# A routed expert network: six of eight token tiles moved before the loop starts, running sums by scan, and the later set-up in another order

## The reference, cut to what matters

```python
gates = softmax(xt @ gate_w); top_v, top_i = top_k(gates, 2)      # 8 experts, 2 per token
top_v = top_v / sum(top_v)
h = gelu(einsum('nd,edf->enf', xt, fc_w), approximate=False)      # first block: 128 -> 512 -> 128
eo = einsum('enf,efd->end', h, proj_w)
out = sum(take(eo, top_i) * top_v)
...
gu = einsum('bsd,edh->ebsh', x, w_gate_up); g, u = split(gu, 2)   # fourth block: 128 -> 2 x 512 -> 128
expert_out = einsum('ebsf,efd->ebsd', silu(g) * u, w_down)
return einsum('bse,ebsd->bsd', gate_probs, expert_out)
```

## Time and profile before

| what | value |
|---|---|
| median of three runs | 620.51 us |
| profiled execution, its own time | 617.3 us |
| its span in the profile | 615.6 us |
| PE busy | 537.0 us (87%) |
| DVE busy | 410.1 us (67%) |
| POOL busy | 272.4 us (44%) |
| ACT busy | 239.9 us (39%) |
| mean granted TensorE clock | 0.926 of full |

### The profile page before, as it was taken

How to read it: one execution, slowest core, us unless ns; L and a number is a source line. 1 busy time by engine, 2 the same in 40 slices (tenths; PEclk the granted TensorE clock), 3 DMA queues, 4 the chain that set the end, 5 groups by cost and what they waited for, 6 DMA issues and landing times.

```text
span 615.6 us, 12275 instructions
## 1 busy us (share of the span) xinstructions
PE 537.0 (87%) x3780; PEld 456.0 (74%) x3781; DVE 410.1 (67%) x1482; ACT 239.9 (39%) x551; POOL 272.4 (44%) x505
## 2 busy tenths in 40 slices
PE   4999866998899899999999798989974399999992
PEld 2678553987896599898977675757763199999992
DVE  8878846322357885456689869888887556555573
ACT  3455233543454434444423233455531043334330
POOL 4464373888758108900000010546436368774332
PEclk9999657999997899999989989999995599999996
DMA  9998011322253100000000720004001112221233
GB/s 304 380 311 266 10 52 37 84 73 69 70 163 107 58 1 1 2 1 1 1 1 2 219 56 2 0 2 138 1 2 39 48 50 71 60 61 52 77 109 120
DMA packets 48153, 47.66 MB, mean 77 GB/s; under 512 B 6470, under 2 KB 37603, under 8 KB 47942
## 3 DMA queue, kind: packets, MB, share of 16 engines
q1 hardware_dynamic: 43558, 37.68, 20.5%
q0 software_dynamic: 4544, 9.38, 4.5%
HBM read 27.53 MB, written 19.51 MB: 76 GB/s over the span
## 4 chain that ended last, share of the span: by engine, by line
PE 73%; DVE 20%; issue 4%; ACT 1%; DMA 1%; another core or an unknown queue 1%; DVEq 0%; POOLq 0%; POOL 0%; SPq 0%; ACTq 0%
PE bank L2391 17%; PE bank L2402 10%; PE bank L1987 8%; PE bank L2183 4%; PE bank L2228 4%; PE bank L2267 4%; PE bank L2256 2%; PE bank L1976 2%; PE bank L1977 2%; PE bank L1978 2%; PE bank L1868 2%; PE bank L2325 1%; PE bank L2379 1%; PE bank L2218 1%; DVE stats L1095 1%
## 5 line engine op out<-in xcount | busy, mean ns | idle before, releaser
L2391 PE MATMUL bank<-xT,wcur 128*128 128x128 f32 x936 | 118.6, 277 | 6.6 <-ACT xT L880 3.6
L2391 PEld LDWEIGHTS bank<-xT,wcur 128*128 128x128 f32 x936 | 110.6, 192 | 10.0 <-issue 5.5
L627 POOL TENSOR_SCALAR var_eps<-mv 128x4 f32<-128x4 f32 (+2 forms) x12 | 2.8, 236 | 183.3 <-DVEq L1813 95.8
L684 POOL DMA_INDIRECT yt<-Y,dest_i x62 | 61.3, 989 | 50.7 <-ACT Y L896 32.0
L668 POOL DMA_INDIRECT xw<-XW,slot_i x64 | 63.3, 989 | 43.3 <-ACT xT L880 10.9
L1445 DVE COPY wcur<-WA 128x512 f32 x78 | 36.3, 466 | 50.3 <-PE bank L2391 26.4
L964 ACT ACTIVATE hT<-bank,b_cols 128x512 f32<-128x512 f32 x64 | 44.0, 688 | 63.1 <-PE bank L1978 62.5
L1987 PE MATMUL bank<-WC,hT 128*128 128x128 f32 x512 | 64.1, 280 | 0.0
L1987 PEld LDWEIGHTS bank<-WC,hT 128*128 128x128 f32 x512 | 61.7, 195 | 1.4
L1583 DVE SCALAR_TENSOR_TENSOR X<-bank,G,X 128x128 f32<-128x128 f32 x128 | 36.0, 343 | 32.7 <-PE bank L1987 27.4
L1460 DVE TENSOR_TENSOR hT<-gb,bank 128x512 f32<-128x512 f32 x39 | 26.8, 688 | 41.7 <-ACT gb L885 39.5
(11 more groups left out here) (406 smaller groups left out, 1182.6 us busy)
## 6 DMA issues: line engine op xcount, KB each, us to landing
xw<-pad_rows SPq DMA_DIRECT2D x34, 260.0 KB, 4.4
xrow<-xw SPq DMA_DIRECT2D x78, 65.0 KB
WA<-in_fc_dram SPq DMA_DIRECT2D x16, 256.0 KB, 4.7
YT<-yt SPq DMA_DIRECT2D x16, 256.0 KB, 3.6
WA<-in_pj_dram SPq DMA_DIRECT2D x8, 256.0 KB, 5.2
WB<-in_fc_dram SPq DMA_DIRECT2D x8, 256.0 KB, 4.9
WB<-in_pj_dram SPq DMA_DIRECT2D x8, 256.0 KB, 6.3
X<-in_x_dram SPq DMA_DIRECT2D x2, 512.0 KB, 4.4
```

The source lines that it names most:

```text
L684: pool.indirect_dma_start(out=yt_dram, out_offset=bass.IndirectOffsetOnAxis(ap=dest_i[:, t:t + 1], axis=0), in_=y_slot(layer, t), in_offse ...
L2391: ins = pe.matmul(dst, wcur[:, s4, at:at + P], xT[s4 % 2][:, :], start=True, stop=True)
```

## The change

It does five things.

1. The moves of group 0 are counted by two semaphores: the first six token tiles (SOON, both choices, 12 moves) and the last two (4 moves). The order of the moves is tile by tile with both choices. The loop's table gets a sixth kind, tiles that are filled by these six token tiles, and SP loads the first five loop tiles (SOON_ONLY is 5) after 12 moves instead of 16. The table has 48 segments.
2. Running sums are made by one `tensor_tensor_scan` in place of the doubling steps: in `choices` over 64 bf16 numbers in place of L1312 to L1315, in `table` over 48 f32 numbers in place of the copy, the six steps and a subtraction. The scan runs on over the experts, so PE takes off what came before with two more matmuls (`minus_bf`) in each `ranks`. The copy of the logits (L1305) goes: DVE reads them from PSUM.
3. `table_out` stands before the last reduction of `places`, not behind the `routed` cast.
4. The later set-up in layer 0 stands otherwise: on PE the bias row before `ranks(0)`, half of the values behind it, two of the four score matrices ahead of `ranks(1)`, the other two and the keys behind the table; ACT's 16 key copies come before the first group's exponents; DVE fetches the first four weights ahead of the masks of the values, and splits the bias row after the loop's counts.
5. PE no longer waits for `most_moved`; it warms with 0 matmuls in layer 0 (before 8) and 14 in layer 1 (before 26). POOL in layer 0 no longer waits for the set-up matmul between group 0 and group 1: a pause stands there.

```diff
 
+SOON = 6
+SOON_ONLY = -(-(SOON * P * TOPK - PARTIAL) // P)
 FIRST_ONLY = -(-(GT * P * TOPK - PARTIAL) // P)
 THREE_ONLY = -(-(GT * P * TOPK * 3 // 2 - PARTIAL) // P)
...
-KINDS = 5
+KINDS = 6
+
+COUNTED = ((SOON - 1, GT - SOON), (GT // 2 - 1, GT // 2))
...
+WARM = 14
...
-                sp.wait_ge(scattered[0], 16 * MOVES * (layer + 1))
+                sp.wait_ge(scattered[0], 16 * TOPK * SOON * (layer + 1))
                 for t in range(SLOTS):
+                    if t == SOON_ONLY:
+                        sp.wait_ge(scattered[1], 16 * TOPK * (GT - SOON) * (layer + 1))
                     if t == FIRST_ONLY:
-
-                        sp.wait_ge(scattered[1], 16 * (MOVES // 2) * (layer + 1))
+                        sp.wait_ge(scattered[2], 16 * (MOVES // 2) * (layer + 1))
                     if t == THREE_ONLY:
-                        sp.wait_ge(scattered[2], 16 * (MOVES // 2) * (layer + 1))
+                        sp.wait_ge(scattered[3], 16 * (MOVES // 2) * (layer + 1))
...
                 for tile in range(GT):
-                    scatter(layer, 0, tile, 0)
-                for tile in range(GT):
-                    scatter(layer, 0, tile, 1)
-                    if tile == GT // 2 - 1:
-                        pool.sem_inc(most_moved, 1)
-                pool.wait_ge(scattered[0], 16 * MOVES * (layer + 1))
+                    for choice in range(TOPK):
+                        scatter(layer, 0 if tile < SOON else 1, tile, choice)
+                pool.wait_ge(scattered[0], 16 * TOPK * SOON * (layer + 1))
                 if layer == 0:
-                    pool.wait_ge(setup_mm, B + 4 + B - 1)
+                    pause()
                 else:
                     pool.wait_ge(ex_xc, SLOTS + 1)
                 pool.wait_ge(routed, GROUPS * layer + 2)
                 for tile in range(GT, GT + GT // 2):
                     for choice in range(TOPK):
-                        scatter(layer, 1, tile, choice)
+                        scatter(layer, 2, tile, choice)
                         pause()
                 if layer == 0:
                     for tile in range(GT + GT // 2, TILES):
...
+                act.wait_ge(s1_mm, 2)
+                act.activation(kT3, bank[4][:, P:2 * P].rearrange("p (b k) -> p b k", b=B), ACT.Identity,
+                               bias=bk3).then_inc(s1_evac, 1)
                 act.activation(kT[:, :, :], bank[4][:, 0:P].rearrange("p (b k) -> p b k", b=B), ACT.Identity,
                                bias=bk1).then_inc(s1_evac, 1)
-                act.wait_ge(s1_mm, 2)
+                act.wait_ge(s1_evac, 1)
+                for h in range(H):
+                    ins = act.activation(kbd[:, :, h, :], kT3, ACT.Copy, scale=head_mask[:, h:h + 1])
+                ins.then_inc(s1_evac, 1)
...
+            for b in range(GB):
+                later_m(b)
+            router(1)
+            for b in range(GB, B):
+                later_m(b)
             later_keys()
-            router(1)
-            later_m()
...
-                link(dve.tensor_copy(lg[:, :, :], logits))
-                two_best()
+                two_best(logits)
...
-                link(dve.tensor_tensor(both[:, g, :, :], oh1[:, :, :], oh2[:, :, :], ALU.add))
-
-                link(dve.tensor_tensor(ahead_a[:, g, PAD + 1:, :], both[:, g, 1:, :], both[:, g, 0:GT - 1, :], ALU.add))
-                link(dve.tensor_copy(ahead_a[:, g, PAD, :], both[:, g, 0, :]))
-                link(dve.tensor_tensor(ahead_b[:, g, PAD:, :], ahead_a[:, g, PAD:, :], ahead_a[:, g, PAD - 2:-2, :], ALU.add))
-                dve.tensor_tensor(ahead_a[:, g, PAD:, :], ahead_b[:, g, PAD:, :], ahead_b[:, g, 0:GT, :],
-                                  ALU.add).then_inc(both_ready, 1)
-                dve.tensor_tensor(dl[:, :, :], lg[:, :, :], m1[:, :].unsqueeze(2).broadcast_to(flat), ALU.subtract)
+                link(dve.tensor_tensor(both[:, g, :].rearrange("p (e t) -> p t e", e=E), oh1[:, :, :], oh2[:, :, :], ALU.add))
+                dve.tensor_tensor_scan(upto_tile[:, g, 2:], both[:, g, :], ones_f[:, 0:E * GT], 0.0,
+                                       ALU.add, ALU.mult).then_inc(both_ready, 1)
...
+                    if g and k:
+                        table_out(layer)
...
-                link(dve.tensor_copy(cum_b[:, pad:], lens[:, :]))
-                src, dst = cum_b, cum_a
-                for step in (1, 2, 4, 8, 16, 32):
-                    link(dve.tensor_tensor(dst[:, pad:], src[:, pad:], src[:, pad - step:pad - step + SEGMENTS], ALU.add))
-                    src, dst = dst, src
-                cum = src[:, pad:]
-                link(dve.tensor_tensor(upto[:, :], cum, lens[:, :], ALU.subtract))
-                link(dve.tensor_tensor(value[:, 0, :], flat_ends[:, 0:SEGMENTS], upto[:, :], ALU.subtract))
+                link(dve.tensor_tensor_scan(cum[:, 1:], lens[:, :], ones_f[:, 0:SEGMENTS], 0.0, ALU.add, ALU.mult))
+                upto, past = cum[:, 0:SEGMENTS], cum[:, 1:]
+
+                rows = slice(0, SLOTS)
+                dve.tensor_tensor(value[:, 0, :], flat_ends[:, 0:SEGMENTS], upto, ALU.subtract)
...
+                dve.wait_ge(experts_known, layer + 1)
                 dve.wait_ge(in_experts[layer], 16 * (len(ups) + 1) * E)
                 for t in range(RING):
                     weights(t)
+                if layer == 0:
+                    values(1)
                 shares(layer, 1)
                 destinations(0)
-                done_counts(layer, tile_counts[layer])
+                done_counts(layer)
+                if layer == 0:
+                    split_row()
                 for t in range(SLOTS):
                     if layer == 1:
...
-                pe.matmul(rank, before_bf[:, :], both[:, g, :, :].rearrange("p t e -> p (t e)"), start=True, stop=False)
-                pe.matmul(rank, ones_bf[:, :], ahead_a[:, g, PAD - 1:-1, :].rearrange("p t e -> p (t e)"),
-                          start=False, stop=True)
-                pe.matmul(count, ones_bf[:, :], ahead_a[:, g, PAD + GT // 2 - 1::GT // 2, :],
-                          start=True, stop=True).then_inc(rank_mm, 1)
+                def by_tile(a):
+                    return a.rearrange("p (e t) -> p t e", e=E)
+
+                ahead, reached = (by_tile(upto_tile[:, g, i:i + E * GT]) for i in (1, 2))
+                start = ahead[:, 0:1, :]
+                pe.matmul(rank, before_bf[:, :], by_tile(both[:, g, :]), start=True, stop=False)
+                pe.matmul(rank, ones_bf[:, :], ahead, start=False, stop=False)
+                pe.matmul(rank, minus_bf[:, :], start.broadcast_to([P, GT, E]), start=False, stop=True)
+                pe.matmul(count, ones_bf[:, :], reached[:, COUNTED[g][0]::COUNTED[g][1], :], start=True, stop=False)
+                pe.matmul(count, minus_bf[:, :], start.broadcast_to([P, 2, E]), start=False, stop=True).then_inc(rank_mm, 1)
...
             def router(layer, n, gate_w):
                 if layer == 0:
                     later_context()
+                    later_row()
                 ranks(layer, 0)
+                if layer == 0:
+                    pe.wait_ge(dl_ready, 1)
+                    values(1, wv3, range(GB))
                 transposes(n, range(GB, B))
                 logits(n, range(GT, TILES), gate_w)
                 if layer == 0:
-                    later_keys()
+                    later_m(0)
+                    later_m(1)
                 ranks(layer, 1)
                 if layer == 0:
-                    values(1, wv3)
-                    later_row()
+                    values(1, wv3, range(GB, B))
                 table(layer)
                 if layer == 0:
-                    later_m()
+                    later_m(2)
+                    later_m(3)
+                    later_keys()
...
-                pe.wait_ge(most_moved, layer + 1)
-                warm((8, 26)[layer], 2)
+                warm((0, WARM)[layer], 2)
                 if layer == 0:
                     pe.wait_ge(m_evac, 2 * B)
+                    pe.wait_ge(s1_evac, 8)
                     pe.wait_ge(setup_evac, B + 3)
```

147 lines of the change are left out of this document (67 added, 80 removed).

## The result

| what | before | after |
|---|---|---|
| median of the runs | 620.56 us (4 runs, 618.83 to 622.11) | 611.92 us (4 runs, 610.50 to 615.25) |
| ratio after to before | | 0.9866, 95% interval 0.9835 to 0.9897 |
| profiled execution, its span | 617.3, 615.6 us | 612.42, 610.2 us |

The change saves 8.6 us by the medians and 5.4 us between the two profiled spans. I had forecast 605.0, that is -15.5, in a range of 598 to 611. In these two profiles the gain is in layer 1 (7.2 us); in layer 0 nothing arrives.

What follows compares the result with a forecast made beforehand. It took the chain from routing through DVE's small dependent steps and PE's set-up or warm-up to the loop's matmuls as the bound. Layer 0 -6.4 and layer 1 -9.1 gave -15.5 from 620.5: 605.0 us, range 598 to 611.

Steps and rivals of the forecast that it cites:

- Scans, ranks, choices: Routing: one scan of 0.3 us replaces a copy and four steps per group, net -0.85 us a group.
- Table: Table on DVE: eight of 18 links go; layer 0's output comes at 92.4, 6.4 us before the 98.83 of now.
- Start of the loop, layer 0: Set-up ahead of layer 0's loop: the first transpose comes at 96.4 instead of 104.72.
- POOL and the end of layer 0: Layer 0's loop: POOL's later moves start 8.2 us earlier, late hand-overs stay until tile 16, the end moves by -6.4 us.
- Layer 1: Layer 1's loop start: earlier numbers, shorter warm-up and earlier loads start the first up matmul sooner, -9.1 us.
- D: Rival: layer 0's loop never leaves the disturbed state of late hand-overs, +15.4 there, 627 us; chance 0.03.
- A: Rival: layer 0's disturbed state of late hand-overs ends with the sixteen moves, sum -19.5, 601 us; chance 0.20.
- B: Rival: a shared port lock makes each DVE step beside a POOL move late, sum -12, 608.5 us; chance 0.14.
- C: Rival: layer 1's short warm-up does not carry and its loop starts at 1.2 GHz, -11, 609.5 us; chance 0.11.
- E: Rival: group 1's moves land late, the loop waits at tile 9 and gives all back, 619 us; chance 0.02.

Runs made afterwards that it cites:

- after_ctl: The changed kernel plus SyncE's assertions that its 16 loaded counts per layer lie in bounds, as baseline: 612.45 us, 0.9879 of the kernel before.
- all16: The changed kernel with assertions; in both layers SyncE starts the loop's loads after all 16 first-half moves instead of 12: 614.47 us, 0.9815.
- ctl2: The changed kernel with the assertions once more, as baseline on chip 3: 613.57 us, 0.9810 of the kernel before.
- table_late: The changed kernel with assertions and 20 more chained copies ahead of the table's scan in both layers: 622.60 us, 0.9949.
- paced16b: paced16 again, on chip 4: 613.92 us, 0.9820 of the kernel before.
- warm0: The changed kernel with assertions, without the 14 warming matmuls in layer 1: 614.33 us, 0.9809.
- pause19: wait_tile with layer 0's pauses longer (memset of 700 instead of 192 elements a row): 622.81 us, 0.9958.
- wait_tile: The changed kernel with assertions; in layer 0 GpSimd waits between the halves' moves for ScalarE's copy of the first turned tile: 608.71 us, 0.9805.
- paced16: The changed kernel with assertions and a pause behind each of layer 0's first 16 moves: 607.90 us, 0.9804.
- own4: The changed kernel with assertions; each of layer 0's first 16 moves waits until the move four before it has landed: 613.32 us, 0.9810.
- rest13: wait_tile, with GpSimd in layer 0 also waiting before its first result until ScalarE has written 13 results: 619.52 us, 0.9914.
- no_pause: The changed kernel with assertions and no pause at all in layer 0: 619.42 us, 0.9915.
- before_pause: The kernel before with assertions; layer 0's GpSimd wait between the halves' moves replaced by one pause: 616.80 us, 0.9961.
- ctl3: The changed kernel with the assertions again, as baseline on chip 4: 613.88 us, 0.9844 of the kernel before.

## Why the prediction was wrong

*Scans, ranks, choices: right.* The scans take 0.29 and 0.26 (taken 0.3). A cost that I had left out came with them: `both`, now written by expert and then by tile, takes 0.43 to 0.48 instead of 0.22 to 0.28. Group 0 was forecast 0.3 later and came 0.4 earlier (73.33 against 73.73), as the bias row did not hold PE. The table began at 83.57 (forecast 84.3).

*Table: right, and a little better.* Layer 0 `entries` at 86.45 (forecast 88.7), since the shorter table was through before the late hand-overs began; the numbers known at 89.4 (92.4).

*Start of the loop, layer 0: this step failed.* "The first transpose comes at 96.4 instead of 104.72." I priced a late hand-over at 0.7 to 0.8 us, the size of the rows of before, and counted only DVE's. In the profile after ACT's hand-overs of the same set-up cost 3.6 and 9.4 us, and the first transpose came at 108.29. The size is no constant, and the forecast's own finding, that POOL "now gets no idle time between the two groups", should have been applied to this stretch too, where ACT's copies stand, and not only to the loop.

*POOL and the end of layer 0: failed as well, and this is the deeper one.* "I take it that it stays: the loop goes at 2.71 a tile from result 0" to tile 16. In the profiled execution the state left when the loop began late, and the loop was even. More important, the term took the early start as a gain at the end. Over the profiles the loop's start lies between 96.9 and 108.7, while the last result of the changed kernel, with or without paced moves and rests of the start, lies 113.2 to 120.0 us after the first move: before it was 117.3. The four profiles that began after 106 us without an edit to POOL or the table (the kernel after, after_ctl, all16, ctl2) have 117.6 to 120.0, the seven that began by 101.5 with the loop's pauses and results as they were have 113.2 to 118.2. An early loop meets POOL's close transfers and is slowed, a late one is not. Forecast -6.4, found +1.8 in the profile and, counted from the first move, between -1.0 and +2.2 in four profiles of the changed kernel and its baseline. That is the missing 5 to 9 us.

*Layer 1: the mechanism was right, the size 2 us off.* Forecast -9.1, found -7.2. The first up matmul was to come 21.0 us after the first move and came after 23.1: the warm-up began 16.4 us after it instead of 14.9, took 4.83 us instead of 4.5, and the second tile's load came 1.11 us behind it. table_late shows that the numbers pass to the start: 7.8 us more of table cost it 5.5. The warm-up's length hangs on the clock that PE has by then: granted 0.65 in these 4.83 us, and 0.51 in paced16b, where the 14 matmuls took 6.05. The 1 to 2 us for a load to land came from no row; warm0 shows 2.3 from issue to transpose. The 0.75 us by which the first group was to be sooner do not show: from layer 0's last write to layer 1's first move it is 274.0 us, before 273.8, in a spread of 271.5 to 275.6 over the profiles.

*Sum.* +1.8 - 7.2 = -5.4, the difference of the spans; forecast were -6.4 - 9.1 = -15.5. The medians have -8.6; the profiled execution of before was 3.3 below its median, that of after 0.5 above. The base was thus a lucky execution, and I had said so, but it does not explain the miss.

*Rivals.* D's premise, that a POOL without rest keeps the state, was tested for the loop: there it leaves by itself when results hold POOL at 1.89 us a write. A did not happen before the loop: ACT was late until 107.33, 13.5 us after the end of the sixteenth move. B did not happen: layer 0's table ran clean. Nor is its rule the cause of the late hand-overs: a lock held for one instruction of POOL, of at most 1.21 us in that stretch, does not make ACT 9.36 us late, and in pause19 POOL's memsets were two and a half times as long (0.69 against 0.27 us), and the slow stretch went away (a memset only writes, so this tests the writing alone). C did not happen as such: the warm-up carried. E, nearly excluded, happened in part where the loop began early: PE waited for tile 9 for 1.12 us in wait_tile, 2.60 in paced16 and 3.34 in pause19. The Trainium skill (SBUF — State Buffer, section SBUF: two separate sides), from which B's lock came, also says that a DMA cannot be slowed by a compute operation, nor the reverse. As to ports no run here speaks against it. In these traces, though, engines that have their data start up to 9.4 us late while POOL issues indirect transfers 1.26 to 1.52 us apart.

*What stays open.* Why instructions start late. That a semaphore is seen late can't be all of it, since DVE's instructions without a wait were late too (0.99 and 1.12 us above; 1.15 and 1.09 in all16). A late supply of instructions is not shown either: the trace after has one packet of the instruction queues at 87.69 and the next at 109.38, and the late instructions between started without one; no run tested it. It is not the number of transfers under way (own4), nor the writing of the port's memsets (pause19). Whether it is the issuing or the traffic of the completions I did not separate. Nor is it known why one chip turned the earlier start into 4 us and another into nothing, nor why the slow stretch returned after six transfers in rest13 and after more than twenty in wait_tile.

## What to carry to other kernels

Before a step's gain is added to the sum, ask what runs beside the time that it moves into: an early start into a stretch that slows everything is a loan. Where one engine issues small indirect transfers closely, price the hand-overs of all engines in that stretch, not only of the one on the chain, and try their spacing (in the loop here 1.94 us was harmless, 1.52 was not) before the order of the work. And where two semaphores race within a microsecond, one profile shows one of two executions: take a second one before building a forecast on it.

## What the runs showed of the hardware

- Late starts go with close indirect transfers of POOL (128 rows of 520 or 512 bytes). At 1.26 us apart they began after some ten transfers. Single ones reached 8.1 us at that spacing (no_pause), and 9.36 when transfers 1.52 us apart followed without a rest (the profile after). At 1.52 us they began after six (rest13, behind a rest of 10.06 us) to more than twenty (wait_tile) and cost a tile of the loop 1 to 4 us. At 1.89 us none were seen in over 60 us (the profile after), at 1.94 none between 124 and 169 us (pause19). They touched ACT, DVE and PE, DVE's chains onto itself, and instructions that wait for nothing.
- Ahead of layer 0's loop rests of POOL of 3.2 to 5.3 us ended them, rests of up to 1.1 us did not. In the loop they also ended about when POOL first waited for a result (161.38 in the kernel before, 135.05 in ctl3).
- In the one place where it can be read (before_pause, 95.68) the transfers were not late meanwhile: the last of 16 had landed 1.39 us after POOL's instruction ended.
- A scan of 64 bf16 numbers a row takes 0.29 us, of 48 f32 numbers 0.26.
